# Moving one of four clamped decay differences to VectorE and spreading the convolution taps in a Mamba-2 decoder layer

## The reference, cut to what matters

```python
proj = hidden_states @ W_in.T                      # z, xBC and dt side by side
xc = causal depthwise convolution of xBC with 4 taps, plus conv_b
xBC = silu(xc)                                      # x, B and C side by side
dt = softplus(dt + dt_bias);  A = -exp(A_log)
dA = dt * A;  A_cum = cumsum(dA)
Lmat[l, s] = exp(A_cum[l] - A_cum[s])  for s <= l, else 0     # per head
y[l] = sum_s (C[l] . B[s]) * Lmat[l, s] * dt[s] * x[s] + D * x[l]
g = y * silu(z)
out = (g * rsqrt(mean(g*g) + eps) * norm_w) @ W_out.T
```

## Time and profile before

| | |
|---|---|
| runs | 1664.83, 1665.1, 1670.2 us; median 1665.1 us |
| the profiled execution | span 1663.1 us from its first to its last instruction, 2.0 us under the median; a time of its own beside the span is not given |
| TensorE busy | 1592.4 us, 96% of the span |
| VectorE busy | 1248.2 us, 75% |
| ScalarE busy | 1202.6 us, 72% |
| GpSimd busy | 819.6 us, 49% |
| mean granted TensorE clock | 0.988 of 2.4 GHz |

### The profile page before, as it was taken

The page is one execution under the profiler, slowest core; times in us unless marked ns, Lnnn a source line. Parts: engine busy times, 40 slices in busy tenths (PEclk is TensorE's granted clock), DMA queues, the critical chain, the costliest instruction groups (busy, mean ns, idle before and its releaser), DMA issues. The chain is left out here.

```text
span 1663.1 us, 29165 instructions
## 1 busy us (share of the span) xinstructions
PE 1592.4 (96%) x9876; PEld 1281.1 (77%) x9876; DVE 1248.2 (75%) x1954; ACT 1202.6 (72%) x2512; POOL 819.6 (49%) x673
## 2 busy tenths in 40 slices
PE   4999999999999999999999999999969999999999
PEld 3777777777777777777777667877758889999888
DVE  6899999999898999998899656766566534433355
ACT  5999899999999999999999566766624334443331
POOL 5677786555555555555565422211124563335460
PEclk8999999999999999999999999999979999999999
DMA  7555555444444454464442100000215333222231
GB/s 283 187 173 176 188 177 165 152 149 156 156 160 145 152 166 167 154 247 154 170 158 89 57 1 14 14 14 27 96 67 178 128 108 108 93 93 93 78 100 52
DMA packets 76239, 209.85 MB, mean 126 GB/s; under 512 B 9152, under 2 KB 32960, under 8 KB 74304
## 3 DMA queue, kind: packets, MB, share of 16 engines
q1 hardware_dynamic: 70432, 181.90, 32.1%
q0 software_dynamic: 5664, 26.09, 4.5%
HBM read 170.99 MB, written 36.96 MB: 125 GB/s over the span
## 5 line engine op out<-in xcount | busy, mean ns | idle before, releaser
L1021 PE MATMUL banks<-pair_hi,m_wxz 128*128 128x512 f32 x1024 | 352.4, 405 | 3.8 <-DVE pair_lo L674 2.3
L749 DVE SCALAR_TENSOR_TENSOR m_xc<-banks,m_cw,m_xc 128x510 f32<-128x510 f32 (+2 forms) x384 | 285.7, 744 | 12.5 <-ACT m_xc L503 2.6
L387 POOL TENSOR_TENSOR m_mat<-m_mat,m_cb_off 128x512 f32<-128x512 f32 x128 | 166.4, 1300 | 220.4 <-DVE m_mat L761 211.4
L517 ACT ACTIVATE m_mat<-m_a_all,m_cum 128x256 f32<-128x256 f32 x512 | 260.0, 508 | 1.6 <-PE m_ps_y L1062 1.6
L1078 PE MATMUL m_ps_out<-m_won,m_gT 128*128 128x256 f32 x1024 | 242.6, 379 | 4.8 <-POOL m_gT L396 3.3
L1021 PEld LDWEIGHTS banks<-pair_hi,m_wxz 128*128 128x128 f32 x1024 | 194.0, 189 | 42.6 <-issue 2.7
L396 POOL TENSOR_TENSOR m_gT<-m_gy,m_zs 128x512 f32<-128x512 f32 x128 | 166.9, 1304 | 106.5 <-DVE m_gy L791 106.2
L1078 PEld LDWEIGHTS m_ps_out<-m_won,m_gT 128*128 128x128 f32 x1024 | 191.7, 189 | 35.8 <-POOL m_gT L396 5.4
L520 ACT ACTIVATE m_mat<-m_a_all,m_cum 128x128 f32<-128x128 f32 x512 | 204.5, 399 | 0.0
L1021 PE MATMUL banks<-pair_lo,m_wxz 128*128 128x512 f32 x512 | 201.1, 393 | 0.0
L1062 PE MATMUL m_ps_y<-m_mat,m_xdt 128*64 128x256 f32 (+1 forms) x2048 | 194.7, 332 | 0.0
(11 more groups left out here) (350 smaller groups left out, 3432.3 us busy)
## 6 DMA issues: line engine op xcount, KB each, us to landing
m_a_all<-a_by_head SPq DMA_DIRECT2D x128, 512.0 KB, 4.0
m_wxz<-w_split SPq DMA_DIRECT2D x96, 512.0 KB, 4.8
w_split<-m_wxz SPq DMA_DIRECT2D x32, 512.0 KB, 3.0
raw<-in_w_gate_up POOLq DMA_DIRECT2D x9, 1280.0 KB, 6.7
raw<-in_w_xz SPq DMA_DIRECT2D x32, 256.0 KB, 4.0
raw<-in_w_down POOLq DMA_DIRECT2D x9, 640.0 KB, 7.7
x_sorted<-f_gT_hi SPq DMA_DIRECT2D x1, 4992.0 KB, 16.2
f_xg<-x_sorted SPq DMA_DIRECT2D x39, 128.0 KB, 2.3
```

The lines of the kernel that those rows point to most:

```text
L387: pool.tensor_tensor(off, off, cb_off[:, g * BG:(g + 1) * BG, :].rearrange("p b t -> p (b t)").unsqueeze(1) .broadcast_to([P, HPT, BG * P] ...
L517: act.activation(first_rows(u, h, b), a_all[u][:, h, b * SEQ:(b + 1) * SEQ].rearrange("p (j t) -> p j t", t=P), ACT.Relu, bias=cum[:, t, h ...
L749: dve.scalar_tensor_tensor(out=out[:, :, k:], in0=ps[:, :, 0:SEQ - k], scalar=cw[:, c, TAPS - 1 - k:TAPS - k], in1=out[:, :, k:], op0=ALU. ...
L1021: last = pe.matmul(ps[:, :], w, a, start=m == 0, stop=m == len(terms) - 1)
```

## The change

Three edits. First, the pair (h, b) = (1, 1) leaves ScalarE's `gaps`; VectorE forms it in a new function `gap(n)` with two `tensor_scalar` instructions (add the per-partition sum, then max with 0). `decays` and `a_load` wait for it as well. Second, the sums are stored negated (`scale=-1.0` in `aT_copy`), so that both engines add. Third, VectorE's list is laid out anew: `conv_x` is called once for each tap, and other work stands between the taps.

```diff
+    GAP_DVE = (1, 1)
...
+        def gap_parts(n, h, b):
+            g, u, head = n // NCT, n % 3, n % NCT * HPT + h
+            t = g % 2 * TPG + 2 * b
+            return (a_all[u][:, h, b * SEQ:(b + 1) * SEQ].rearrange("p (j t) -> p j t", t=P),
+                    cum[:, t, head:head + 1], a_all[u][:, h, b * SEQ + P:(b + 1) * SEQ],
+                    cum[:, t + 1, head:head + 1])
...
                     sp.wait_ge(gap_done, HPT * (n - 2))
+                    sp.wait_ge(gap_dve_done, n - 2)
...
-                act.activation(aT[:], ps_s[:, 0:SEQ], ACT.Copy).then_inc(aT_done, 1)
+                act.activation(aT[:], ps_s[:, 0:SEQ], ACT.Copy, scale=-1.0).then_inc(aT_done, 1)
...
                 for b in range(BG):
+                    if (h, b) == GAP_DVE:
+                        continue
+                    rows, first, late, later = gap_parts(n, h, b)
+                    act.activation(first_rows(u, h, b), rows, ACT.Relu, bias=first)
+                    last = act.activation(later_rows(u, h, b), late, ACT.Relu, bias=later)
                 last.then_inc(gap_done, 1)
...
             def decays(n):
                 act.wait_ge(gap_done, HPT * (n + 1))
+                act.wait_ge(gap_dve_done, n + 1)
...
-            def conv_x(n):
+            def conv_x(n, k):
                 c = n % NCT
-                dve.wait_ge(x_scaled, n + 1)
+                if k == 1:
+                    dve.wait_ge(x_scaled, n + 1)
+                else:
+                    dve.wait_ge(conv_step, n * CONV + k - 1)
...
+            def gap(n):
+                u = n % 3
+                dve.wait_ge(a_loaded[u], 16 * (n // 3 + 1))
+                if n % NCT == 0:
+                    dve.wait_ge(cum_done, n // NCT + 1)
+                if n >= 3:
+                    dve.wait_ge(y_ready, n - 2)
+                rows, first, late, later = gap_parts(n, *GAP_DVE)
+                dve.tensor_scalar(first_rows(u, *GAP_DVE), rows, first, 0.0, ALU.add, ALU.max)
+                dve.tensor_scalar(later_rows(u, *GAP_DVE), late, later, 0.0, ALU.add, ALU.max).then_inc(gap_dve_done, 1)
...
-            conv_x(0)
+            for k in range(1, TAPS):
+                conv_x(0, k)
+            gap(0)
+            gap(1)
...
             for n in range(N):
                 turned = n % NCT == 1 and n > 1
+                more = n + 1 < N
                 if n >= 1:
                     gate(n - 1)
                 if turned:
                     mean_out(n // NCT - 1)
+                if more:
+                    conv_x(n + 1, 1)
                 if n >= 1:
                     x_times_dt(n)
-                if n + 1 < N:
-                    conv_x(n + 1)
+                if more:
+                    conv_x(n + 1, 2)
+                if n + 2 < N:
+                    gap(n + 2)
                 if turned:
                     add_out(n // NCT - 1)
                 if n < N - NCT:
                     prepare_next(n)
+                if more:
+                    conv_x(n + 1, 3)
```

More of the change, by code:

```diff
@@ L185, in mamba_phase @@
             sem(n) for n in ("x_scaled", "gap_done", "exp_done", "x_tanh", "z_tanh", "g_squared"))
-        mat_off = sem("mat_off")
+        mat_off, gap_dve_done = sem("mat_off"), sem("gap_dve_done")
         (conv_step, x_silu, z_silu, xdt_done, mat_done, gy_done, g_done, sum_mean, x_added) = (
@@ L513, in gaps @@
                         act.wait_ge(y_ready, n - 2)
-                head = c * HPT + h
                 for b in range(BG):
[L516 to L521, removed]
+                    if (h, b) == GAP_DVE:
[3 more added lines that the diff above has]
+                    last = act.activation(later_rows(u, h, b), late, ACT.Relu, bias=later)
                 last.then_inc(gap_done, 1)
@@ L742, in masked @@
                 dve.tensor_tensor(cb_diag[:, h % 2 * BG + b, :], ps_s[:, 0:2 * P], mask[:], ALU.mult).then_inc(cb_done, 1)
-            def conv_x(n):
+            def conv_x(n, k):
                 c = n % NCT
-                dve.wait_ge(x_scaled, n + 1)
+                if k == 1:
+                    dve.wait_ge(x_scaled, n + 1)
+                else:
+                    dve.wait_ge(conv_step, n * CONV + k - 1)
                 out, ps = batches(xc[:, n % 2, :]), batches(ps_x[n % 2][:, :])
[L748 to L754, removed]
+                dve.scalar_tensor_tensor(
+                    out=out[:, :, k:], in0=ps[:, :, 0:SEQ - k],
+                    scalar=cw[:, c, TAPS - 1 - k:TAPS - k], in1=out[:, :, k:],
+                    op0=ALU.mult, op1=ALU.add).then_inc(conv_step, 1)
+            def gap(n):
[8 more added lines that the diff above has]
+                dve.tensor_scalar(later_rows(u, *GAP_DVE), late, later, 0.0, ALU.add, ALU.max).then_inc(gap_dve_done, 1)
             def matrices(n):
@@ L902, in _ @@
                     silu_z(1)
-                elif n + 1 < N:
+                elif more:
                     matrices(n + 1)
```

## The result

The changed kernel takes 1759.2 us (median of 4 runs, 1757.69 to 1760.24), beside 1664.96 for the kernel before (4 runs, 1663.78 to 1670.2) on the same chip. The ratio is 1.0561, with an interval of 1.0546 to 1.0575: slower by 94 us, where 80 were forecast.

A forecast was written before the change was run, and what follows sets the result against it. TensorE was taken to set the pace at 6.52 us a step, VectorE in round 0; a 6.89 us loop plus preparing and 14 us of block added 79.5 to 1663.1, giving 1742.6, and 1745 as median; range 1700 to 1780.

The forecast's parts named there:

- a loop of 6.89 us a step: Scale of x, taps with x_times_dt and pair between, tanh to next scale: 6.89 us, over TensorE's 6.52; before, 6.06.
- VectorE's wait at the first tap: In a steady step VectorE, with 6.11 us of its own, waits 0.78 us for ScalarE's scale of x.
- ScalarE's wait at tanh: ScalarE waits about 1.2 us a step at tanh_x for the third tap, so the 0.69 saved becomes a wait.
- The steady pair: In a steady step the pair starts 3.37 us after the gate's start, GpSimd's L407 ending at 3.39: called just clear.
- the faster case: Rival: the loop does not close, TensorE's 6.52 stays the pace, round 0's idle time goes: 12 to 17 us, 1650; chance 0.04.
- The preparing does not hide: Denies the rival that next-round work falls into the loop's waits: some 1683 us, or 1669 without the block; chance 0.08.
- The pair at the dearer rate: Rival: VectorE's pair runs at single rate, 0.66 us, and is held: 7.08 a step, 1783; chance of over 1775: 0.08.
- SyncE's load: SyncE's load now waits for VectorE's pair too, with two steps in hand until the data is used: costs nothing.
- the block in round 0: GpSimd's L407 holds VectorE's pair 1.05 us in each of 27 steps, 28 us, or nothing; half, 14, taken.
- The price of a hold: VectorE's pair held by GpSimd: 1.05 us a step in round 0, 0.80 in a steady step without the tap wait.
- both ways a steady step is 6.9: Steady step: the loop gives 6.89 us; without the tap wait, VectorE's 6.11 plus a 0.80 hold gives 6.91.
- The start: Kernel start, with two pairs on VectorE before the first silu: counted as nothing within 1 us.

The follow-up runs named there:

- The run with the pair earlier: The changed kernel with VectorE's pair moved one place up, ahead of the second tap: 1808.29 us, ratio 1.0858.
- the order alone: The changed kernel with its VectorE order kept (taps laid apart) but all four pairs on ScalarE: 1697.43 us, ratio 1.0198.
- the three others that move the pair: The changed kernel with the third tap ahead of prepare_next (1738.73 us), pair ahead of the second tap (1808.29), or pair behind taps and prepare_next (1685.23).
- the pair alone: The changed kernel with the pair still on VectorE, but the three taps together again and the pair right behind them: 1691.42 us, ratio 1.0157.

## Why the prediction was right, and which terms were off

**The mechanism held, term by term.** The forecast was a loop of 6.89 us a step; it is 6.86. VectorE's wait at the first tap was put at 0.78 and is 0.70; ScalarE's wait at tanh at 1.2 and is 1.10; the pair at 0.34 and 0.28 shown and 0.47 on the list, and it is 0.34, 0.28 and 0.46 (945.23 to 945.69). TensorE was to idle 0.4 a step at its transposes and shows 0.28. The steady pair was to come just clear of GpSimd, though its own figures put it 0.02 us ahead of the end (3.37 against 3.39). It starts at 945.23, and GpSimd's timeline shows

```profile
943.95 1.29 POOL L416 TENSOR_TENSOR m_g_sum<-m_g_sum,m_g_sq 128x512 f32<-128x512 f32 x1
```

which ends at 945.24, 0.01 behind the pair's start. The pair takes its 0.34 all the same: a held instruction ends 0.15 us behind GpSimd's (below), and this one ends later than that on its own. The experiments show the cause, beyond the match of the sums: take the pair out of the loop and the plain step is 6.52 again; leave the order and take the pair away, and it is 6.52 too; put the pair where it is held, and it is 7.45.

**The rivals.** The loop closes in every plain step, so the faster case fails. The preparing does not hide: as long as it stands ahead of the third tap it lengthens its step to some 7.6 us, and one place later the held pair takes back two thirds of what was to be won. The pair at the dearer rate fails by its row of 0.34. SyncE's load was costed at nothing. Its queue still waits, now for VectorE's pair: 600.1 us in 112 times over the four rounds, against 547.0 in 96 for ScalarE's over those of before. VectorE's pair waited 0.2 us in all for the data that it loads (the second row of L772 below). ScalarE's exp needs VectorE's pair too and shows no wait for it, and the copy that negates the sums takes 0.37 to 0.38 us, as before.

**The terms that were off.** By the same windows the rounds were to grow by 25.8, 23.0, 20.3 and 10.4, together 79.5, and grew by 95.4 with the start. The difference is 7.1, 1.3, 2.4, 2.6 and 2.5 for the start. The loop itself came out 0.03 us shorter than forecast, some 4 us over 126 steps, so the other terms were off by that much more; that the two partly cancel is luck.

The largest is the block in round 0: 28 us or nothing, taken as half. VectorE's lines in round 0, and over the whole kernel:

```profile
L772 DVE TENSOR_SCALAR m_mat<-m_a_all,m_cum 128x256 f32<-128x256 f32 x31 | 31.4, 1014 | 0.0
...
L772 DVE TENSOR_SCALAR m_mat<-m_a_all,m_cum 128x256 f32<-128x256 f32 x128 | 66.5, 520 | 0.2 <-DMA m_a_all<-a_by_head 0.2
```

Held for 1.014 - 0.344 = 0.67 us in each of 31 steps, it cost 20.8 us, not 14: 6.8 of the 7.1 by the size. One such instruction on VectorE:

```profile
192.73 1.39 DVE L772 TENSOR_SCALAR m_mat<-m_a_all,m_cum 128x256 f32<-128x256 f32 x1
```

and GpSimd's instruction, which it outlasts by 0.15 us:

```profile
192.69 1.28 POOL L416 TENSOR_TENSOR m_g_sum<-m_g_sum,m_g_sq 128x512 f32<-128x512 f32 x1
```

The prediction let 0.09 us decide between the whole hold of 1.05 and none. What came is 0.64 of it, as a mean over 31 steps, where half over 27 steps was taken. This sizes round 0 by VectorE's own rows; TensorE's busy time there rose by 6.9 us as well (the clock, below), and no run parts the two. The price of a hold was also too high by the prediction's own rows: a held instruction ends 0.15 us behind GpSimd's, so the pair in round 0 is held for 6.93 + 0.15 - 5.76 - 0.34 = 0.98, and in a steady step without the wait for 3.39 + 0.15 - 2.59 - 0.34 = 0.61, not 0.80. VectorE's step would then be 6.72, and "both ways a steady step is 6.9" does not come out; the loop's 6.89 does not rest on it. The run with the pair earlier bears this out: 0.66 us from the pair's start to the end of GpSimd's instruction, 0.47 of hold. The Trainium skill, SBUF — State Buffer, section "SBUF: two separate sides", says that the two engines share a pair of ports, and that when a VectorE instruction in a two-port mode meets one of GpSimd, the one that starts first keeps the pair for its whole length while the other waits. The three held instructions shown here, and their ends 0.15 us behind GpSimd's, agree with it.

The start was counted as nothing within 1 us and cost 2.5. In the kernel with the order alone it costs -0.4, in the three others that move the pair and in the pair alone 1.0 to 1.9, so the early pairs on VectorE have part in it; how the 2.5 divide was not measured. In round 3 step 101 grew from 8.3 to 10.05 us, 1.4 more than the 0.37 that the sum gives a step. TensorE waits there for a weight load behind the next phase's loads, 2.07 us where it waited 1.51 before, and a stretch at half clock follows (below). Step 101 took 7.45 to 12.0 in the kernels of this study, with waits of 0.42 to 3.67 for that load; what sets the wait stays open. Of the 2.4 of round 2 some 1.2 are the clock, below.

## What to carry to other kernels

Before work is moved or spread between engines that run in order, add up the loop from one instruction to its successor in the next step through both lists: a list that has slack, like VectorE's 0.56 us, gives it only outside that loop, and work put between its links costs its whole length once the loop is over the pace of the bound engine. Relief of an engine that is not the bound turns into a wait; here 0.69 us of it a step was worth 2 us in all. And an instruction of VectorE that GpSimd can hold belongs where nothing waits for it, since its hold moves with every wait that is removed ahead of it.

## What the runs showed of the hardware

No change of the clock was expected, and there were some. In the changed kernel seven stretches of some 3.4 us inside the Mamba-2 steps, four of them in round 0, one in round 2 and two in round 3, run at half clock; the kernel before showed none from 46 to 1213 us. TensorE's first instruction ahead of one of them, which stood idle for 2.10 us:

```profile
110.77 0.66 PE L1078 MATMUL banks<-ident,m_xs 128*128 128x128 f32 x4 [2.10 <-DVE m_xs L785]
```

The window of 2 us behind it, where the granted clock is 0.50, the lower of the two levels (1.2 GHz); the columns are those of the windows above:

```profile
112.00:114.00 2.00, 2.00 (x6) 1.59 (x5) 0.81 (x3) 2.00 (x5) 1.94 (x3) 0.50 0.01 4
```

Ahead of another, near 562 us, TensorE had idled for 1.04. Each makes a step's twelve projections 4.4 us long in place of 2.8. In round 0 this is mostly hidden, as VectorE and ScalarE set the pace and the steps with a stretch are as long as their neighbours, 8.6 to 9.0 us; the step behind the stretch at 562 us took 8.70, with VectorE's gate waiting 1.76 for TensorE's scan, where the same step of the round before took 7.54, so some 1.2 us are lost there. Of the two in round 3 one, at 832 us, is in step 101, behind its wait of 2.07, and makes the projections 1.6 us longer; what the other, at 801 us, costs was not measured. Waits of TensorE can thus have a second price, but it is a few us of the 94. Which waits bring it the traces don't show: in the four rounds TensorE idled for 1 us or more 44 times, where it had done so 5 times before.
